# One transformer decoder layer on one core: both context loads of a batch are issued by ScalarE instead of by SyncE

## The reference

```python
x = x + attn(layernorm(x), wq, wk, wv, wo)    # 8 heads of 128, RMS norm and rotary embedding on q and k, causal softmax
x = x + xattn(layernorm(x), ctx, ctx)         # h = x @ ctx.T (375 rows); gelu(h) @ ctx, both products per batch
x = x + ffn(layernorm(x), w1, b1, w2, b2)     # 256 -> 1024 -> 256, inputs and weights rounded to 8 bits, ReLU
```

## Time and profile before

| | |
|---|---|
| median of 3 runs | 654.29 us (653.25 to 656.85) |
| the profiled execution's own time | 654.7 us |
| span of its trace, first to last instruction | 652.9 us |
| busy PE / DVE / ACT / POOL, share of the span | 91% / 90% / 83% / 53% |
| mean granted TensorE clock | 0.974 of full speed |

### The profile page before, as it was taken

The page is one execution under the profiler, slowest core; times in us unless marked ns, Lnnn a source line. Parts: engine busy times, 40 slices in busy tenths (PEclk is TensorE's granted clock), DMA queues, the critical chain, the costliest instruction groups (busy, mean ns, idle before and its releaser), DMA issues.

```text
span 652.9 us, 13103 instructions
## 1 busy us (share of the span) xinstructions
PE 593.3 (91%) x4624; PEld 477.3 (73%) x4624; DVE 588.1 (90%) x1339; ACT 543.0 (83%) x1402; POOL 348.0 (53%) x430
## 2 busy tenths in 40 slices
PE   1746889999999999999999999999999999997864
PEld 1424667777887788888778877888887788776753
DVE  3768899999999999999999999999999999998442
ACT  6675788999999999989998899999889999998522
POOL 1134555665555565666655555656666555556111
PEclk9967999999999999999999999999999999999978
DMA  8071566766776766667687676666677777666451
GB/s 296 0 200 36 114 139 138 137 138 150 149 148 137 147 133 142 141 141 153 133 151 152 143 152 138 137 142 132 143 149 138 150 152 146 134 141 138 89 109 37
DMA packets 222641, 88.92 MB, mean 136 GB/s; under 512 B 200704, under 2 KB 217552, under 8 KB 222320
## 3 DMA queue, kind: packets, MB, share of 16 engines
q1 hardware_dynamic: 222576, 88.08, 63.6%
HBM read 34.84 MB, written 3.67 MB: 59 GB/s over the span
## 4 chain that ended last, share of the span: by engine, by line
DVE 75%; ACT 9%; PE 5%; POOL 3%; issue 3%; DMA 3%; SPq 0%; ACTq 0%; DVEq 0%
DVE turn_s L433 11%; DVE turn_c L425 8%; DVE qk L524 8%; DVE o L550 5%; DVE ss L566 5%; DVE turn_c L614 5%; DVE ss L603 5%; DVE qk L639 4%; DVE h_t L590 2%; DVE y_out L545 2%; DVE g L628 2%; DVE x L634 2%; DVE stat L534 1%; POOL turn_c L354 1%; DVE xn L600 1%
## 5 line engine op out<-in xcount | busy, mean ns | idle before, releaser
L912 PE MATMUL psum<-wqkv,xT 128*112 128x512 f16 x384 | 148.3, 386 | 12.5 <-DMA xT<-xn 9.1
L913 PE MATMUL psum<-wqkv,xT 128*112 128x512 f16 x384 | 147.4, 384 | 0.0
L914 PE MATMUL psum<-wqkv,xT 128*112 128x512 f16 x384 | 147.1, 383 | 0.0
L354 POOL TENSOR_TENSOR turn_c<-turn_c,turn_s 112x1024 f32<-112x1024 f32 x32 | 75.7, 2365 | 48.4 <-DVE turn_s L433 48.4
L912 PEld LDWEIGHTS psum<-wqkv,xT 128*112 128x112 f16 x384 | 50.7, 132 | 43.4 <-DMA xT<-xn 9.7
L425 DVE TENSOR_TENSOR turn_c<-psum,cos_t 112x1024 f32<-112x1024 f32 x64 | 77.8, 1215 | 0.0
L433 DVE TENSOR_TENSOR turn_s<-psum,sin_t 112x1024 f32<-112x1024 f32 x64 | 77.7, 1214 | 0.0
L914 PEld LDWEIGHTS psum<-wqkv,xT 128*112 128x112 f16 x384 | 50.7, 132 | 34.1 <-issue 1.9
L922 PE MATMUL psum<-wo,oT 128*112 128x256 f16 x256 | 71.0, 277 | 4.7 <-DMA oT<-o 3.5
L524 DVE SCALAR_TENSOR_TENSOR qk<-turn_c,rms,qk 112x128 f16<-112x128 f32 x256 | 69.2, 343 | 2.6 <-ACT qk L796 2.5
L924 PE MATMUL psum<-wo,oT 128*112 128x256 f16 x256 | 71.0, 277 | 0.0
(11 more groups left out here) (107 smaller groups left out, 1699.2 us busy)
## 6 DMA issues: line engine op xcount, KB each, us to landing
ctxT<-in_ctx_cols SPq DMA_DIRECT2D x32, 375.0 KB, 3.4
ctx_in<-in_ctx_rows SPq DMA_DIRECT2D x32, 375.0 KB
x_in<-in_x SPq DMA_DIRECT2D x32, 112.0 KB, 2.3
out_y<-y_out SPq DMA_DIRECT2D x32, 112.0 KB, 2.9
w_raw<-in_w SPq DMA_DIRECT2D x2, 1024.0 KB, 6.1
w_raw<-in_wk SPq DMA_DIRECT2D x2, 512.0 KB, 5.0
w_raw<-in_wq SPq DMA_DIRECT2D x2, 512.0 KB, 6.5
w_raw<-in_wv SPq DMA_DIRECT2D x2, 512.0 KB, 8.2
```

What stands on the lines that cost most here:

```text
L354: pool.tensor_tensor(turn_c[:, 1, :], turn_c[:, 1, :], turn_s[:, 1, :], ALU.add).then_inc(k_turned, 1)
L912: pe.matmul(dst, hi, wqkv[:, 0, c, w, cols], start=c == 0, stop=False)
L913: pe.matmul(dst, hi, wqkv[:, 1, c, w, cols], start=False, stop=False)
L914: last = pe.matmul(dst, lo, wqkv[:, 0, c, w, cols], start=False, stop=c == MC - 1)
```

## The change

Both context loads leave SP's list. `load_ctx` now stands in ACT's list between `tanh_h` and `scale_k1`, for batch `Batch(i - 2)`, and `load_ctxT` between `normalise_o0` and `round_o`, for `Batch(i - 1)`. What is loaded, the buffers, the semaphores and their counts stay as they are. No wait is added or removed.

```diff
@@ SP @@
-            def load_ctxT(j):
-                sp.dma_start(ctxT[:, j.off % 2], ctx_cols[j.at].rearrange("o (c p) s -> (o p) c s", p=P)).then_inc(
-                    ctxT_landed[j.off % SLOTS], 16)
...
-            def load_ctx(j):
-                sp.dma_start(ctx_in[:, j.off % 2], ctx_rows[j.at].rearrange("o (p c) m -> (o p) c m", c=SC)).then_inc(
-                    ctx_landed[j.off % SLOTS], 16)
...
-                if e.inside(B):
-                    load_ctxT(e)
                 if g.inside(B):
                     transpose_xq(g)
...
                 if d.inside(B):
                     transpose_o(d)
-                if e.inside(B):
-                    load_ctx(e)
                 if a.inside(B):
                     transpose_x(a)
@@ ACT @@
+            def load_ctx(j):
+                act.dma_start(ctx_in[:, j.off % 2], ctx_rows[j.at].rearrange("o (p c) m -> (o p) c m", c=SC)).then_inc(
+                    ctx_landed[j.off % SLOTS], 16)
...
+            def load_ctxT(j):
+                act.dma_start(ctxT[:, j.off % 2], ctx_cols[j.at].rearrange("o (c p) s -> (o p) c s", p=P)).then_inc(
+                    ctxT_landed[j.off % SLOTS], 16)
...
                 if g.inside(B):
                     tanh_h(g)
+                if f.inside(B):
+                    load_ctx(f)
                 if d.inside(B):
                     scale_k1(d)
...
                     normalise_o0(e)
+                    load_ctxT(e)
                     round_o(e)
```

More of the change, by code:

```diff
@@ L291, in body @@
             def body(i):
-                a, c, d, e, g, i = (Batch(i + 3), Batch(i + 1), Batch(i - 0), Batch(i - 1), Batch(i - 3), Batch(i - 5))
-                if e.inside(B):
-                    load_ctxT(e)
+                a, c, d, g, i = (Batch(i + 3), Batch(i + 1), Batch(i - 0), Batch(i - 3), Batch(i - 5))
                 if g.inside(B):
```

## The result

The changed kernel is slower: 662.1 us median of five runs (659.45 to 663.44) against 655.23 us for the kernel before (five runs, 653.25 to 656.85). The ratio is 1.0100, 95% interval 1.0076 to 1.0124. The predicted range (651.5 to 669) holds it. The forecast itself, 655.8 us and no change that can be told, did not come true: what happened is the case that had a chance of 0.31, slower by over half a per cent. One execution of 806 us and one of 1256 us in the series further down are disturbed and left out of their ranges and ratios.

The account below looks back on a forecast made before the run. DVE and PE were taken as full, the chain running 75% through DVE. Zero for SP and both issues plus 1.5 us for q's transpose on the profiled 654.7 gave 656.2, as a median 655.8 us; range 651.5 to 669.

Parts of the forecast that it names:

- SP's relief is worth nothing: SP's list: two issues fewer per batch, 47 us of SP's time over 27 batches, costed at zero; SP already waits 4.7 us per batch.
- The issues cost nothing: ACT's stream: issuing `ctx_in` behind the tanh (0.4 to 0.6 us) and `ctxT` behind o's scaling costs DVE zero.
- `ctxT` in the full stretch: DMA engines, during transposes of k, q and o: `ctxT` delays q by up to 1.2 us; 1.5 us in all, bounds 0 to 4.1.
- the four: Four of 27 q transposes, landing after 5.2 to 6.2 us, expected to make PE wait; 4.1 us together if passed on in full.
- into the slacker stretch, and I cost it at nothing: DMA engines: `ctx_in` moves from behind o to the stretch busy to 0.40, at no cost.
- I am wrong if the batch gets longer than 18.1 us in the middle: Sign against the forecast: longer batches, above all with DVE idle before `split_o` or `split_q`, or PE idle before `scores`.
- The rival that SP holds `ctxT`'s issue: ACT's `ctxT` issue waits behind SP's issues, `round_o` late, 16 to 20 us on DVE: 670 to 674 us; chance 0.13.
- The rival that q is late in every batch: `ctxT` delays q's transpose by 2 us, PE waits 0.75 us per batch, half passed on: 665 us; chance 0.09.

## Why the range held and the forecast was too low

- *SP's relief is worth nothing:* right. SP stands 113.3 us before `xn`'s transpose, as in the earlier trace rows, and the two kernels with both loads off SP and `ctxT` at its old time are no faster than before.
- *The issues cost nothing:* right. `ctx_in`'s took 0.28 us, below my 0.4 to 0.6, `ctxT`'s 0.41. ACT does compute on, and runs further ahead than I took from DVE: the issue of `ctxT` starts at 314.32, with seven of the eight instructions ahead of it not yet started, where I counted four. It therefore comes 0.75 us earlier than I placed it (0.31 us after `rden` begins, not 1.06), while SP is still issuing k's transpose. (Between the tanh and `round_q0` lie nine instructions, not twelve; nothing hung on it.)
- *`ctxT` in the full stretch:* the place is right, the size was at fault. "Passed on in full, the four would cost about 0.7, 1.1, 1.1 and 1.2 us, 4.1 together. Since the chain runs through DVE and not PE, I take 1.5 us of it": alone it measured 3.1 us (2.0 to 4.3). q landed in 4.9 us median, just under the 5 to 5.6 I expected, 0.4 later than before and not 1.2. Four batches waited, but only one of the four that I had counted (that of 332.2, here 335.24), so the agreement is luck; the rows also had four more landings, of 4.7 to 4.9 us, which the same sum would have charged with 0.2 to 0.4 us each. And a chain that runs through DVE was no reason to take less than all. A late q is a late exp, a late `rms` and a late `round_q0`, and DVE, which has no air, waits for that a batch later: in the knot above 1 us of PE's waiting became about 1.5 us of DVE's time. The sum had no term for `x_in`, which moves beside `ctxT` now: DVE waits 1.1 us for it in the run with `ctxT` alone, 1.9 in the changed kernel.
- *`ctx_in` goes "into the slacker stretch, and I cost it at nothing":* this step failed. I read the share of 0.40 as room for it. The share is a mean over 16 engines, and `ctx_in` keeps as much as five of them busy while it moves. The transpose of `xn`, which had landed in 2.4 us, lands in 4.3 beside it (with `ctx_in` split in 2.4 again). The load measured 1.6 us alone (0.8 to 2.5), and in the changed kernel splitting it took 0.59% off, 3.9 us. By which wait it costs is not settled: PE's waits for `xn` are 0.7 us in all, and with `ctxT` at its old time the same late landing cost nothing that shows. PE's waits for ACT's normalisation of o go with it too (5.0 us in 16 batches with `ctx_in` alone on ACT, no entry with it split); why is open.
- With both as measured alone, the median before of 655.2 + 3.1 + 1.6 is 659.9; the median of 662.1 has some 2 us more. That `ctx_in` costs more beside a late `ctxT` (1.6 alone, 3.9 there) would account for it.
- *"I am wrong if the batch gets longer than 18.1 us in the middle"*, above all with PE idle before `scores`: this sign came. From `rden` at 151.82 to that at 568.92 lie 23 batches of 18.13 us on average, 17.96 in the kernel before, and PE stands before `scores` in four.
- *The rival that SP holds `ctxT`'s issue:* no. The longest of the 32 took 0.46 us. The Trainium skill (Perfetto Trace Analysis, "Per-instruction lifecycle") describes a block shared by two sequencers and locked for each DMA; no wait for it shows in ACT's issues here, although SP was issuing beside them. SP's issue of q did grow, to 2.91 us, but it did so with `ctxT` on SP too (2.72 us), so that is no effect of two issuers.
- *The rival that q is late in every batch:* no, PE waits for it in four of 24; with `ctxT` twice it is so in 14 of 23.
- The Trainium skill (DMA: Bandwidth & Descriptors, "Issuing engines are not separate DMA queues") says that DMAs of all issuers interleave on the same 16 engines. The trace agrees for `ctxT` (1.0048 from ACT, 1.0061 from SP). It doesn't follow that the issuer is of no account: with `ctx_in` from ACT at SP's old time, moving side by side is what cost 1.9%, and one queue had kept the order.

Why are only some batches hit? Those that were had a landing of q 1 to 2 us over the median; in the kernel before such landings occur too, and there the margin took nearly all of it. The packet records show what goes with them, which the prediction left aside: packets of 8192 and 16384 bytes on two queues that the page lists as "instruction" (q14, q8). Of q's 24 transposes from 150 to 580 us, those with no such packet under way land in 4.3 to 4.6 us before the change (13 of them) and 4.2 to 5.0 after it (10, median 4.7). All landings above that, up to 6.2 and 6.6 us, have one under way, those of the four batches that waited among them. So `ctxT` takes about 0.3 us of the margin in a usual batch, and PE waits where such a packet comes on top. No run moved these packets, so their part is seen in the records and not tested; with `ctxT` twice, batches without one wait too.

## What to carry to other kernels

Moving a DMA to another engine moves its transfer in time and takes it out of the order of its old queue; both mattered more here than the issuing time saved. Before such a move, find what stands next to it in the new place, and how many DMA engines each of the two uses: a mean share of 0.3 to 0.4 can be five engines that are full. Where two engines are both nearly full, don't discount a wait because the chain runs through the other one: a late input may cost more than its own lateness (1 us became 1.5 here). And list all that will move beside the load in its new place, small loads like `x_in` too.

## What the runs showed of the hardware that I had not expected

ACT's stream runs at least seven instructions ahead to a DMA issue (314.32 us above), in two batches eleven (350.97 and 133.41). The transfer over 125 partitions had its packets mostly five at a time (share 0.29), and cut into 112 and 13 it lets the transpose beside it land in 2.4 us instead of 4.3. A transpose's 256-byte packets took 161 to 189 ns each beside 3072-byte packets of another queue, and 23 ns without. In the kernels before and after, every transpose of q from 150 to 580 us that took more than 5.0 us to land had an "instruction" packet beside it.

POOL's `rms` for q, the same instruction on the same shape, took twice its time in two batches, each right after a late q (source view of its line in the changed kernel, 100 to 580 us, ns min/median/max; in the kernel before all 27 took 1.66 us):

```profile
L369 POOL TENSOR_TENSOR rms<-ms,nhalf x26: 1662/1663/3277, 110.7 to 564.8; 112x8 f32<-112x8 f32 x26
```

Its time goes with how long before DVE's L602 it starts, which in the knot above is 0.22 us (346.28 and 346.50) and in the batch before it 0.75. In the traces of six kernels (before, after, `ctxT` alone on ACT, both at the old times, `ctxT` on SP at the new time, `ctxT` twice) every `rms` for q that starts 0.4 us or more ahead took 1.7 us, those 0.23 to 0.37 ahead 1.8 to 2.0, those 0.18 to 0.22 ahead (four) 3.2 to 3.3, and those 0.12 or less ahead 1.6 to 1.7. Why is not shown.
